# Listing the full halves of a chunk while its later groups still fill it, with four chunks in place of five and outputs written over the sorted rows

## What is computed

```python
ln = layernorm(layernorm(x)); xn = layernorm(ctx)         # each with its own gamma and beta
q = (ln @ Wq + bq) * 128 ** -0.5                          # 8 heads of 128
k, v = split(concat([xn, ln]) @ Wkv + bkv)                # 128 keys per batch element
x = x + tanh(g_xattn) * (softmax(q @ k.T) @ v @ Wo + bo)
t = layernorm(x)
probs = softmax(t @ Wr + br); the two largest are kept as weights cw
x = x + tanh(g_ffn) * sum_e cw[e] * (relu(t @ W1[e] + b1[e]) @ W2[e] + b2[e])
```

## Time and profile before

| what | value |
|---|---|
| median of three runs | 797.29 us (795.64 to 798.03) |
| the profiled execution's own time | 798.88 us |
| its span in the profile | 797.2 us |
| PE busy | 769.3 us, 97% |
| DVE, ACT, POOL busy | 525.8, 495.1, 427.6 us |
| time by SP's queue on the 16 DMA engines | 38.2% |
| read and written in HBM | 34.44 and 40.04 MB |

### The profile page before, as it was taken

How to read it: one execution, slowest core, us unless ns; L and a number is a source line. 1 busy time by engine, 2 the same in 40 slices (tenths; PEclk the granted TensorE clock), 3 DMA queues, 4 the chain that set the end, 5 groups by cost and what they waited for, 6 DMA issues and landing times.

```text
span 797.2 us, 17389 instructions
## 1 busy us (share of the span) xinstructions
PE 769.3 (97%) x5426; PEld 647.4 (81%) x5426; DVE 525.8 (66%) x1820; ACT 495.1 (62%) x1623; POOL 427.6 (54%) x439
## 2 busy tenths in 40 slices
PE   7999999999999999999999999999999999989997
PEld 6778777776889888778988778898877898878775
DVE  5646667595857567677758777766768556566444
ACT  4776677776866566767556576656667665563332
POOL 2233365656542435785655686665568566424551
PEclk9999999999999999999999999999999999999999
DMA  7835152542545532174664136565315556533221
GB/s 197 234 126 192 60 213 87 192 149 78 169 167 181 190 138 71 51 225 159 217 213 125 57 100 216 187 209 182 109 48 169 177 172 204 191 106 90 57 80 54
DMA packets 115069, 116.39 MB, mean 146 GB/s; under 512 B 13961, under 2 KB 90530, under 8 KB 114978
## 3 DMA queue, kind: packets, MB, share of 16 engines
q1 hardware_dynamic: 106880, 100.44, 38.2%
q0 software_dynamic: 7168, 14.69, 6.3%
q10 hardware_dynamic: 930, 0.15, 0.1%
HBM read 34.44 MB, written 40.04 MB: 93 GB/s over the span
## 4 chain that ended last, share of the span: by engine, by line
PE 80%; POOL 5%; issue 5%; DVE 4%; ACT 4%; DMA 1%; SPq 1%; ACTq 0%; DVEq 0%; POOLq 0%
PE shared L1449 13%; PE batch L1387 11%; PE batch L1400 11%; PE hid_ps L1310 8%; PE xy_ps L1324 7%; PE batch L1395 6%; PE batch L1377 3%; PE shared L1233 3%; PE shared L1235 3%; PE shared L1234 3%; ACT probs L757 3%; POOL probs L687 2%; PE xy_ps L1287 2%; POOL yg L677 2%; PE shared L1359 2%
## 5 line engine op out<-in xcount | busy, mean ns | idle before, releaser
L687 POOL TENSOR_TENSOR probs<-probs,rsums 128x512 f32<-128x512 f32 x128 | 132.9, 1038 | 233.0 <-DVE rsums L1163 231.4
L757 ACT ACTIVATE probs<-batch,neg_max 128x128 f32<-128x128 f32 x512 | 180.5, 374 | 2.0 <-DVE neg_max L1167 2.0
L838 ACT ACTIVATE qT<-shared,tb 128x512 f32<-128x512 f32 x128 | 87.2, 696 | 85.6 <-PE shared L1235 74.3
L1400 PE MATMUL batch<-pT_sb,kvn 128*128 128x512 f32 x256 | 133.6, 603 | 2.9 <-ACT pT_sb L765 2.9
L1387 PE MATMUL batch<-kvT,qT 128*128 128x128 f32 x1024 | 135.4, 275 | 0.8 <-ACT qT L838 0.8
L662 POOL DMA_INDIRECT sorted_x<-xn,row_of x112 | 115.3, 1029 | 26.7 <-issue 26.6
L1449 PE MATMUL shared<-M,oT 128*128 128x128 f32 x1024 | 125.5, 276 | 0.3
L1387 PEld LDWEIGHTS batch<-kvT,qT 128*128 128x128 f32 x1024 | 124.4, 192 | 1.2 <-ACT qT L838 1.2
L1449 PEld LDWEIGHTS shared<-M,oT 128*128 128x128 f32 x1024 | 119.4, 192 | 1.7 <-issue 1.6
L757 ACT ACTIVATION_READ_ACCUMULATOR probs<-batch,neg_max 128x1 f32 x512 | 110.2, 215 | 0.0
L1163 DVE RECIPROCAL rsums<-sums 128x4 f32<-128x4 f32 x128 | 22.7, 177 | 131.5 <-ACT probs L757 115.4
(11 more groups left out here) (177 smaller groups left out, 1250.0 us busy)
## 6 DMA issues: line engine op xcount, KB each, us to landing
wt<-wall SPq DMA_DIRECT2D x124, 321.0 KB
sorted_x<-yg SPq DMA_DIRECT2D x36, 512.0 KB, 5.0
xt<-sorted_x SPq DMA_DIRECT2D x147, 64.0 KB
sorted_y<-y_sb SPq DMA_DIRECT2D x71, 128.0 KB
kv<-in_ctx_dram SPq DMA_DIRECT2D x16, 256.0 KB
kv<-in_x_dram SPq DMA_DIRECT2D x16, 256.0 KB
xres<-in_x_dram SPq DMA_DIRECT2D x32, 128.0 KB
out_dram<-x SPq DMA_DIRECT2D x15, 256.0 KB
```

The costliest lines, as they stand in the source:

```text
L687: nc.gpsimd.tensor_tensor(pv, pv, rsums[:, m % 2, :].unsqueeze(2).broadcast_to([P, 4, P]), ALU.mult).then_inc(probs_ready, 1)
L757: last = nc.scalar.activation(probs[:, m % 2, c * P:(c + 1) * P], batch_ps[m % BANKS][:, c * P:(c + 1) * P], ACT.Exp, bias=neg_max[:, m % ...
L838: nc.scalar.activation(qT[:, g % 2, :, number, :], sh[:, :].rearrange("p (b i) -> p b i", b=GB), ACT.Identity, bias=tb[:, number:number + ...
L1400: nc.tensor.matmul(batch_ps[m % BANKS][:, :], kvn[:, m % KVN, :], pT_sb[:, :], start=True, stop=True).then_inc(o_ready, 1)
```

## The change

CHUNKS is now (4, 4, 3, 3), with ROWS = 2048, at most 39, 39, 31 and 31 halves, 140 in all in 72 tiles. For each chunk two tables are made instead of one (LISTED): one after the last but one of its groups, of the halves that are full by then, and one at its end, of all the rest. After m groups at least (2 * 512 * m - 889) // 128 halves are full, rounded to whole tiles: 8 tiles of a chunk of four, 4 of a chunk of three. These can run while the last group is being scattered. Slots of the tiles are now 43 to 62, 75 to 94, 99 to 102, 107 to 118, 123 to 126 and 131 to 142. DVE's `list_halves` (s = 1) makes a list of the halves that are new since the last one, and `open_list` (s = 4) keeps what the second list of a chunk needs.

Every chunk has its own DRAM tensor, `sorted`, of 8 * 2048 rows and 1024 spare ones for halves that do not exist. `store_tile` writes a half's outputs over the rows it was computed from, each half by a DMA of its own with the address that `load_tile` read, so gathers use `row_of` as scatters do, and `find_homes` and the waits for a set's reuse are gone. The four tensors are cleared by 68 DMAs of 512 KB (17 a chunk, in runs of 2 KB where they were 4 KB), spread over slots 1 to 56, and each group's scatter waits for its own part alone. Gathers begin at slot 65, where they began at 61, and the ninth sorted group already takes a late buffer (LATE_GROUP 8, was 9). ACT fetches weights from the 61st tile on. POOL sets a few more constants at the start.

The core of the diff (lines that `list_tiles` had are left out of `list_halves`):

```diff
 
 
 
-CHUNKS = (3, 3, 3, 3, 2)
+CHUNKS = (4, 4, 3, 3)
 SORTED = sum(CHUNKS)
 DENSE = tuple(range(SORTED, G))
 STEPS = E * len(DENSE)
 NCH = len(CHUNKS)
...
+LISTED = ((3, 4), (3, 4), (2, 3), (2, 3))
+
+
+def full_halves(k, m):
+
+    return HALVES[k] if m == CHUNKS[k] else (2 * m * TOK - E * (HALF - 1) + HALF - 1) // HALF
+
+
+LISTS = tuple((k, FIRST_GROUP[k] + m - 1, full_halves(k, m)) for k in range(NCH) for m in LISTED[k])
+N_LISTS = len(LISTS)
+LIST_AT = {g: v for v, (_, g, _) in enumerate(LISTS)}
+
+
+def opens(v):
+
+    return v == 0 or LISTS[v][0] != LISTS[v - 1][0]
+
+
+def closes(v):
+
+    return v + 1 == N_LISTS or LISTS[v][0] != LISTS[v + 1][0]
+
+
+TILES_TO = tuple(FIRST_TILE[k] + (TILES[k] if g == LAST_GROUP[k] else upto // 2) for k, g, upto in LISTS)
+LIST_OF_TILE = tuple(min(v for v in range(N_LISTS) if i < TILES_TO[v]) for i in range(N_TILES))
+LISTED_FROM = (0,) + TILES_TO
+LONGEST = max(HALVES)
+SPARE = E * HALF
...
-FILL = 1024
-FILLS = E * ROWS // FILL
+FILLS = [(k, e, j) for k in range(NCH) for j in range(max(CHUNKS)) for e in ((E, 0, 2, 4, 6) if j == 0 else (0, 2, 4, 6))]
+CLEARING = 56
...
-    for k in range(NCH):
-        n = max(n, GB * (LAST_GROUP[k] + 2) + 7 + AHEAD)
-        for _ in range(TILES[k]):
+    for v, (_, g, _) in enumerate(LISTS):
+        n = max(n, GB * (g + 2) + 7 + AHEAD)
+        for _ in range(LISTED_FROM[v], LISTED_FROM[v + 1]):
...
-LATE_GROUP = min(g for g in range(SORTED) if TILE_SLOT[FIRST_TILE[CHUNK_OF_GROUP[g] + 1] - 1] + 4 >= TAIL)
-BUFFER = [g % 2 if g < LATE_GROUP else (2, 3, LATE_GROUP % 2, 1 - LATE_GROUP % 2)[(g - LATE_GROUP) % 4] for g in range(SORTED)]
+OLDEST_LATE = GB * (G - 1) + 1
...
+LATE_GROUP = min(g for g, n in enumerate(gather_slots(buffers(SORTED))[1]) if n > OLDEST_LATE)
+BUFFER = buffers(LATE_GROUP)
+GATHER_AT, _, GATHER_END, SUMMED = gather_slots(BUFFER)
...
-        xs = [nc.dram_tensor(f"sorted_x{p}", (E * ROWS, D), F32).ap() for p in range(SETS)]
-        ys = [nc.dram_tensor(f"sorted_y{p}", (max(TILES) * TILE, D), F32).ap() for p in range(SETS)]
+        sorted_rows = [nc.dram_tensor(f"sorted{k}", (E * ROWS + SPARE, D), F32).ap() for k in range(NCH)]
...
                 if q == 0:
                     sp.wait_ge(const_step, 7)
-                p, q = q // FILLS, q % FILLS
-                sp.dma_start(xs[p][q * FILL:(q + 1) * FILL, :].rearrange("(p r) d -> p (r d)", p=P), zeros[:, :]).then_inc(cleared[p], 16)
+                k, e, j = FILLS[q]
+                if e < E:
+                    rows_of = sorted_rows[k][0:E * ROWS, :].rearrange("(e r) d -> e r d", e=E)[e:e + 2, j * TOK:(j + 1) * TOK, :]
+                    rows_of = rows_of.rearrange("e (p r) d -> p e (r d)", p=P)
+                else:
+                    rows_of = sorted_rows[k][E * ROWS:E * ROWS + SPARE, :].rearrange("(e p r) d -> p e (r d)", e=2, p=P)
+                sp.dma_start(rows_of, zeros.rearrange("p (e n) -> p e n", e=2)).then_inc(cleared[group_cleared(k, j)], 16)
...
             def load_tile(i):
-                k = CHUNK_OF_TILE[i]
-                t = i - FIRST_TILE[k]
-                if t == 0:
-                    wait_shared(sp, shared_out, "table", LAST_GROUP[k], 0)
-                    wait_rows_scattered(sp, k)
-                if t % AT_ONCE == 0:
-                    read_table(mybir.EngineType.SP, 0, first_rows, i, N_TILES, E * ROWS - HALF)
+                if opens_list(i):
+                    g = LISTS[LIST_OF_TILE[i]][1]
+                    wait_shared(sp, shared_out, "table", g, 0)
+                    wait_rows_scattered(sp, g)
+                if reads_table(i):
+                    read_table(mybir.EngineType.SP, 0, first_rows, i, N_TILES, E * ROWS + SPARE - HALF)
                 wait(sp, xt_ready, i - XB + 1)
                 for a in range(PARTS[i]):
-                    sp.dma_start(xt[:, i % XB, a, :], xs[k % SETS][bass.ds(first_rows[i, a], HALF), :]).then_inc(got_x[i % XB], 16)
+                    sp.dma_start(xt[:, i % XB, a, :], sorted_rows[CHUNK_OF_TILE[i]][bass.ds(first_rows[i, a], HALF), :]).then_inc(got_x[i % XB], 16)
...
-                if t == 0 and k >= SETS:
-                    wait_outputs_gathered(sp, k - SETS)
                 wait(sp, y_done, i + 1)
-                rows_of = ys[k % SETS][t * TILE:t * TILE + PARTS[i] * HALF, :]
-                sp.dma_start(rows_of.rearrange("(a p) d -> p a d", p=HALF), y_sb[:, i % 2, 0:PARTS[i], :]).then_inc(y_stored[i % 2], 16)
+                for a in range(PARTS[i]):
+                    sp.dma_start(sorted_rows[CHUNK_OF_TILE[i]][bass.ds(first_rows.pop((i, a)), HALF), :], y_sb[:, i % 2, a, :]).then_inc(y_stored[i % 2], 16)
...
-                if CLEAR <= n < CLEAR + SETS * FILLS:
-                    clear(n - CLEAR)
+                for q in range(len(FILLS)):
+                    if n == CLEAR + q * CLEARING // len(FILLS):
+                        clear(q)
...
                 if c == 0:
                     pool.wait_ge(placed, g + 1)
-                    pool.wait_ge(cleared[k % SETS], 16 * FILLS)
-                    if k >= SETS:
-                        wait_tiles_read(pool, k - SETS)
+                    pool.wait_ge(cleared[g], cleared_before(g))
                 for choice in range(2):
-                    nc.gpsimd.indirect_dma_start(xs[k % SETS][:, :], bass.IndirectOffsetOnAxis(ap=row_of[:, g, choice, c:c + 1], axis=0),
+                    nc.gpsimd.indirect_dma_start(sorted_rows[k][:, :], bass.IndirectOffsetOnAxis(ap=row_of[:, g, choice, c:c + 1], axis=0),
...
-                    pool.wait_ge(homes_ready, k + 1)
                     for h in in_buffer(BUFFER[g], g - 1)[-1:]:
                         pool.wait_ge(res_done, h + 1)
                     if g == LATE_GROUP:
                         pool.wait_ge(scores_ready, GB * (G - 1))
-                nc.gpsimd.indirect_dma_start(outputs_of(g)[:, c, choice, :], None, ys[k % SETS][0:HALVES[k] * HALF, :],
-                                             bass.IndirectOffsetOnAxis(ap=home[:, g, choice, c:c + 1], axis=0)
+                nc.gpsimd.indirect_dma_start(outputs_of(g)[:, c, choice, :], None, sorted_rows[k][:, :],
+                                             bass.IndirectOffsetOnAxis(ap=row_of[:, g, choice, c:c + 1], axis=0)
...
+            def list_halves(n, s):
 
                 g = n // GB - 2
+                if s == 1 and g in LIST_AT:
+                    v = LIST_AT[g]
+                    k = LISTS[v][0]
+                    nth = v - min(u for u in range(N_LISTS) if LISTS[u][0] == k)
+                    now, kind = nth % 2, 0 if opens(v) else 2 if closes(v) else 1
+                    mine, next_ = (0 if nth == 0 else 1 + nth % 2), 1 + (nth + 1) % 2
+                    cols = 2 + E if closes(v) else 1 + E
+                    new = n_halves[:, now, :] if opens(v) else n_new[:, :]
                     wait_shared(dve, shared_out, "place", g, 0)
+                    nc.vector.scalar_tensor_tensor(out=filled[:, :, :], in0=next_row[:, :].unsqueeze(2).broadcast_to([P, E, J]),
+                                                   scalar=0.0 if closes(v) else 1.0 - HALF, in1=begins[:, :, :],
+                                                   op0=ALU.add, op1=ALU.is_gt).then_inc(table_step, 1)
+                    dve.wait_ge(table_step, TABLE * v + 1)
+                    nc.vector.tensor_reduce(n_halves[:, now, :], filled[:, :, :], AX, ALU.add).then_inc(table_step, 1)
+                    dve.wait_ge(table_step, TABLE * v + 2)
+                    if opens(v):
+                        nc.vector.scalar_tensor_tensor(out=adds[:, mine, 0, 2:2 + E], in0=n_halves[:, now, :], scalar=-float(HALF),
+                                                       in1=leap[:, kind, :], op0=ALU.mult, op1=ALU.add).then_inc(table_step, 2)
+                    else:
+                        nc.vector.tensor_tensor(n_new[:, :], n_halves[:, now, :], n_halves[:, 1 - now, :], ALU.subtract).then_inc(table_step, 1)
+                        nc.vector.scalar_tensor_tensor(out=adds[:, mine, 0, 2:2 + E], in0=n_halves[:, now, :], scalar=-float(HALF),
+                                                       in1=leap[:, kind, :], op0=ALU.mult, op1=ALU.add).then_inc(table_step, 1)
+                        dve.wait_ge(table_step, TABLE * v + 3)
+                    nc.vector.tensor_tensor(n_upto[:, :, :], before[:, 1:E + 1, :], new.unsqueeze(1).broadcast_to([P, E, E]),
                                             ALU.mult).then_inc(table_step, 1)
+                    dve.wait_ge(table_step, TABLE * v + 5)
+                    nc.vector.tensor_reduce(ends[:, 2:2 + E], n_upto[:, :, :], AX, ALU.add).then_inc(table_step, 1)
+                    dve.wait_ge(table_step, TABLE * v + 6)
+                    past = tile_id if opens(v) else since
+                    nc.vector.scalar_tensor_tensor(out=hit[:, :, 0:cols], in0=ends[:, 0:cols].unsqueeze(1).broadcast_to([P, 2, cols]),
```

(20 more changed lines are left out.)

175 lines of the change are left out of this document (72 added, 103 removed).

## The result

The changed kernel takes 801.25 us (median of 12 runs, 799.02 to 802.49), the kernel before 797.34 in the same session (12 runs): ratio 1.0049, 95% interval 1.0036 to 1.0062. It is slower by 3.9 us where 4.4 less was forecast, and outside the range. Its profiled execution took 800.54 us, 0.7 under its median.

The account below looks back on a forecast made before the run. PE's stream was taken to set the pace in tile slots and nearly so elsewhere. Terms -6.3 + 0.9 - 0.7 + 0 + 1.0 + 0.7 gave -4.4 us, a median of 792.9, range 789.5 to 797.5.

Parts of the forecast that it names:

- Step 7: SP and POOL queues: two stores a tile add 0.4 us of SP time, hidden by the weights' lead, so nothing.
- Steps 1 and 2: PE work: 7 halves fewer before slot 131, -6.3 us; three more tables, one transpose each, +0.9 us.
- rival (d): Tile slots: POOL or ACT pace them, so only a part is saved: -2 us, 795.3; chance 0.06.
- Step 3: Slot 36: without the home operations on DVE, PE's wait for a projection bank read goes, -0.7 us.
- Step 4: Gaps without tiles: PE's waits move with them and the table's copy is met oftener; net 0, -1.5 to +1.5 us.
- Step 5: First two tiles' weights: one clearing DMA ahead of each fetch makes them late, +1.0 us, from 0 to above 4.
- rival (a): Slots 43 to 56: clearing holds up weights in most slots, +8.7 us instead of +1.0, 800.6; chance 0.08.
- Step 6: End of attention, slots 127 to 130 without tiles: the last elements' bare chain costs +0.7 us, 0 to 2.
- Rival (b): Slots 128 to 131: idle PE brings one more half-clock stretch and 2 us of bubble, 795.9; chance 0.2.
- four signs that I named against myself: Weight waits beyond slot 45, waits at listed groups' fourth slots, a second half-clock stretch, tile slots no longer gapless.

Follow-up runs that it names:

- old_chunks_aligned: Changed kernel's code with the earlier kernel's chunks and lists, clearing in slots 1 to 38, table rows padded to 256 bytes at the memory's start: 795.02 us, ratio 0.9972.
- after_aligned: Changed kernel with only the table moved to the start of on-chip memory, rows of 256 bytes instead of 156: 791.66 us, ratio 0.9935 to the kernel before.
- clear38_aligned: Changed kernel with its 68 clearing transfers in slots 1 to 38 and table rows padded to 256 bytes at the memory's start: 792.45 us, ratio 0.9939.
- before_32fills: Kernel before with 32 more 512 KB transfers of zeros, in slots 37 to 56, into rows that nothing reads: 800.81 us, ratio 1.0046.
- clear42: Changed kernel with its 68 clearing transfers spread over slots 1 to 42 instead of 1 to 56: 800.26 us, ratio 1.0045 to the kernel before.
- two_queues: Changed kernel with the 24 or so clearing transfers of slots 37 to 56 issued by ScalarE on its own queue: 797.59 us, ratio 1.0002.
- clear38: Changed kernel with its 68 clearing transfers in slots 1 to 38 instead of 1 to 56: 798.04 us, ratio 1.0014 to the kernel before.
- seven_last: Changed kernel, clearing in slots 1 to 38, third chunk listed once, last 20 tiles beside attention four slots later (bare slots 107 to 110): 797.14 us, ratio 1.0004.

## Why the prediction was wrong

**Step 7 is the step that failed.** It said "SP's weights lead by twelve us in the middle of a chunk (233.94 to 246.2 again), so nothing", and counted SP's transfers alone. It left out what SP does beside issuing: 33 reads of the table, each about 1.15 us longer in all lists but two (the one ahead of slot 51's fetch 2.2). What it put at nothing cost 9.6 us, together with the clearing and the second stores that share the queue. The new shape of the table is one line of the diff, and no step spoke of it; in the kernel before half of the reads took 0.53 us and the longest 1.51, and they stood in its trace as a thing that could be priced. The lead of 12 us was also near the best of a chunk: in slots 49 to 58 of the kernel before, fetches were issued 8.0 to 12.6 us before use, the least for slot 51, and late reads, a clearing transfer and a second store use that up together.

**Steps 1 and 2** (-6.3 + 0.9 = -5.4) were right: PE's busy time fell by 4.8 us, 57 records as counted, and with fast reads slots 35 to 63 had PE idle for 1.3 us only (rival (d) is out). **Step 3** (-0.7): slot 36 got 1.0 us shorter. But old_chunks_aligned, which has the new code and not the new chunks, was 1.7 us faster than the kernel before. In its profile the wait in the tail is 1.32 us where it was 2.07, which no step forecast.

**Step 4** (0, between -1.5 and +1.5): in after_aligned PE stands 6.5 us for 5.2 in slots 64 to 126, +1.3, inside its bound. With the slow reads it was +2.8, of which 1.57 is the wait at slot 107.

**Step 5** (+1.0): a miss of place. The first two tiles didn't wait at all; slots 51 to 59 did, 2.9 us, by the mechanism of rival (a), a fetch behind more work than its lead. But this clearing alone does not do it: with fast reads it costs nothing (after_aligned against clear38_aligned). Denser clearing does, 1.6 transfers a slot in before_32fills, 4.0 us with fast reads. Here it was a load on a queue that was already late. The Trainium skill's rule that step 5 cited (DMA: Bandwidth & Descriptors, section Queues, rings and completion order) agrees with two runs: transfers just ahead of the first fetch held it up for 3.14 us (clear42), and taken out of its queue they left 0.7 us of the later waits (two_queues).

**Step 6** (+0.7, 0 to 2): from the last scores to the second late tile's hidden matmuls it takes 14.8 us in after_aligned (682.38 to 697.22) and 15.2 in the changed kernel (688.55 to 703.75) where 14.2 were forecast: +1.3 and +1.7, inside the bounds. Outside that stretch lies the wait at slot 135, 2.49 us, since ScalarE's read of 1.85 us stands before its copy of the weights. Rival (b)'s second stretch of half clock didn't come in the profile. In the other executions something like it did: the mean granted clock of 0.9953 is 0.0022 under the 0.9975 that 17 executions of the kernel before had beside after_aligned, about one stretch more (an estimate), and a part of what after_aligned won back.

So the change as written missed the forecast by a cause outside all my cases. After_aligned took 5.1 us off the kernel before beside it, near the forecast 4.4, but partly by luck: steps 1, 2, 4, 5 and 6 came to -3.7 for the chunks and lists, which gave 2.6 to 3.4, and the rest of the change was put at 0.7 and gave 1.7. Of the four signs that I named against myself, waits on weights beyond slot 45 came, and with them tile slots that were no longer gapless.

## What to carry to other kernels

When a tensor that an engine reads into registers changes its shape, look at where its rows begin, and keep them on 16 bytes or more: here one padded table was worth more than all the work that the change removed, on a queue that other things had made short of time. Price the queue engine's own instructions (register reads, waits) as you price its transfers, since a lead of some us is eaten by several small things and each of them then looks like the cause. When two unrelated edits each win back the same few us, look for what they both relieve before you keep either.

## What the hardware showed that I had not expected

- A register read of up to eight 4-byte words from on-chip memory takes about 0.53 us at the least where its row begins 0, 496 or 624 bytes into its tensor, and at least 1.49, mostly 1.67 or more, where it begins 124, 156, 248, 312 or 372 bytes in. The bound is 16 bytes by these offsets: 248 and 312 are multiples of 8 and slow, 496 and 624 aren't multiples of 32 and are fast. These are the rows' starts, counted from the tensor's own; where the tensor itself began no run shows. The Trainium skill (Runtime: NRT & Kernel Launch, section Instruction fetch mechanics) puts such loads, there from HBM, at about 200 ns a register, which makes 1.6 us for eight (an estimate). The slow rows here come near that, the fast ones are a third of it.
- Stretches at half clock (1.2 GHz) followed PE waits of 2.07 us (kernel before), 2.49 (changed kernel), 2.31 (before_32fills) and 3.14 us (clear42), and one of 1.90 us in clear38, where the wait of 2.48 us later had none behind it. So the length of the one wait doesn't decide. The profiles of clear38, seven_last and two_queues have one in the first 35 us too, in a part where those of the kernel before and of the changed one have none.
- Transfers of zeros moved from SP's queue to ScalarE's gave back 3.7 us at the same total traffic, with ScalarE busy 62% of the span.
